# The mixer's convolution moved from TensorE, VectorE and ScalarE to GpSimd, with rows shifted by transfers inside the chip

## The reference

```python
x = x + 0.5 * ffn(layernorm(x), gate_weight, wi, wo)
n = layernorm(x)                                   # n_t: row of token t
t = conv_w[:,0]*n_{t-1} + conv_w[:,1]*n_t + conv_w[:,2]*n_{t+1} + conv_b   # per channel, zero beyond a batch's ends
u, v  = n @ Wu.T + bu, n @ Wv.T + bv
gates = sigmoid(relu(n @ Wg1.T + bg1) @ Wg2.T + bg2)
x = x + t + (cumsum(u*gates, axis=1) * (v*gates)) @ Wu
x = x + 0.5 * ffn(layernorm(x), gate_weight, wi, wo)
```

## Time and profile before

| | before |
|---|---|
| median of 3 runs (lowest to highest) | 1102.23 us (1101.32 to 1102.9) |
| the profiled execution's own time | 1102.27 us |
| its span | 1100.5 us |
| its granted TensorE clock | 0.973 |
| mixer, first transposition to its last products | 463.85 to about 656 us |

### The profile page before, as it was taken

How to read it: one execution, slowest core, us unless ns; L and a number is a source line. 1 busy time by engine, 2 the same in 40 slices (tenths; PEclk the granted TensorE clock), 3 DMA queues, 4 the chain that set the end, 5 groups by cost and what they waited for, 6 DMA issues and landing times.

```text
span 1100.5 us, 20918 instructions
## 1 busy us (share of the span) xinstructions
PE 1050.6 (95%) x7912; PEld 994.7 (90%) x7912; DVE 721.7 (66%) x1089; ACT 544.2 (49%) x851; POOL 147.0 (13%) x135
## 2 busy tenths in 40 slices
PE   8699999999999999599999996999999999999995
PEld 6699999999999999478777776999999999999995
DVE  7566566766677777388685874557767677665652
ACT  4445454665556575253333234355656656554431
POOL 2201111113020210100000022002112021130101
PEclk9699999999999999899999996999999999999998
DMA  8458646566465651500011235346566564654410
GB/s 307 175 229 287 204 142 216 182 232 211 166 211 185 243 198 55 177 1 1 1 39 39 77 105 179 128 149 243 178 226 233 193 243 178 227 212 143 170 38 24
DMA packets 83277, 177.33 MB, mean 161 GB/s; under 512 B 4192, under 2 KB 4704, under 8 KB 83168
## 3 DMA queue, kind: packets, MB, share of 16 engines
q1 hardware_dynamic: 75488, 152.61, 39.5%
q0 software_dynamic: 7168, 23.07, 5.9%
q10 hardware_dynamic: 576, 1.05, 0.3%
HBM read 162.04 MB, written 18.87 MB: 164 GB/s over the span
## 4 chain that ended last, share of the span: by engine, by line
PE 93%; ACT 1%; DMA 1%; DVE 1%; issue 1%; POOL 1%; POOLq 0%; SPq 0%; ACTq 0%; DVEq 0%
PE psH L1213 13%; PE psH L1212 13%; PE psH L1214 13%; PE acc L1220 12%; PE acc L1221 12%; PE acc L1219 12%; PE acc L1212 3%; PE acc L1214 3%; PE acc L1213 3%; PE psT L1428 1%; PE psT L1267 1%; PE psH L1340 1%; PE acc L1384 1%; PE psH L1384 1%; PE psT L1533 1%
## 5 line engine op out<-in xcount | busy, mean ns | idle before, releaser
L1212 PE MATMUL psH<-dth,wih 128*128 128x240 f32 (+5 forms) x1024 | 294.2, 287 | 0.0
L1213 PE MATMUL psH<-dtl,wih 128*128 128x240 f32 (+5 forms) x1024 | 293.3, 286 | 0.0
L1220 PE MATMUL acc<-htl,woh 128*128 128x240 f32 (+5 forms) x1024 | 293.3, 286 | 0.0
L1221 PE MATMUL acc<-hth,wol 128*128 128x240 f32 (+5 forms) x1024 | 293.1, 286 | 0.0
L1214 PE MATMUL psH<-dth,wil 128*128 128x240 f32 (+5 forms) x1024 | 293.0, 286 | 0.0
L1219 PE MATMUL acc<-hth,woh 128*128 128x240 f32 (+5 forms) x1024 | 293.0, 286 | 0.0
L786 DVE TENSOR_TENSOR wol<-raw_wo,woh 128x1024 fp32r<-128x1024 f32 x128 | 155.7, 1223 | 146.3 <-ACT woh L608 146.3
L642 ACT ACTIVATE gel<-psH 128x320 f32<-128x320 f32 x256 | 112.0, 437 | 188.3 <-PE psH L1214 183.0
L608 ACT ACTIVATE woh<-raw_wo 128x1024 fp32r<-128x1024 f32 x128 | 134.3, 1057 | 132.2 <-PE acc L1221 132.2
L1212 PEld LDWEIGHTS psH<-dth,wih 128*128 128x128 f32 x1024 | 193.5, 189 | 0.4
L1213 PEld LDWEIGHTS psH<-dtl,wih 128*128 128x128 f32 x1024 | 193.5, 189 | 0.0
(11 more groups left out here) (194 smaller groups left out, 1163.8 us busy)
## 6 DMA issues: line engine op xcount, KB each, us to landing
raw_wi<-in_wi SPq DMA_DIRECT2D x64, 1024.0 KB, 5.1
raw_wo<-in_wo SPq DMA_DIRECT2D x64, 1024.0 KB, 5.3
out_x<-xt SPq DMA_DIRECT2D x4, 1024.0 KB, 5.8
xt<-in_x SPq DMA_DIRECT2D x6, 512.0 KB, 7.8
xt<-x SPq DMA_DIRECT2D x3, 1024.0 KB, 9.7
raw_u<-in_wuT SPq DMA_DIRECT2D x1, 1024.0 KB, 10.9
raw_u<-in_wvT SPq DMA_DIRECT2D x1, 1024.0 KB, 12.6
xt<-in_x ACTq DMA_DIRECT2D x2, 256.0 KB, 3.4
```

The source lines that it names most:

```text
L1212: pe.matmul(out, lh, rh, start=first, stop=False)
L1213: pe.matmul(out, lh, rl, start=False, stop=False)
L1220: pe.matmul(out, lh, rl, start=False, stop=False, skip_group_check=True)
L1221: return pe.matmul(out, ll, rh, start=False, stop=False, skip_group_check=True)
```

## The change

The convolution is computed on the rows with tokens on partitions. A tile's row one token earlier or later lies on the next partition, so SP copies each group's `xn` twice inside the SBUF: into `late` one partition down (127 rows of four tiles) and into `soon` one partition up, with single rows for the edges. GpSimd multiplies `late`, `xn` and `soon` with rows of weights (`conv_row`), adds the bias and the three products and adds the sum to `xt`: 28 operations of 128x512 a group, with waits after each four. `conv_row` is made once, between the layers, by 16 transpositions on TensorE and 4 copies on ScalarE. `conv_mid`, `tap`, `turn_conv` and the first addition of `adds` are gone. `xn` has memory for two groups now, so that `norm(g)` for g >= 2 waits until GpSimd has added group g-2, and `adds(w)` waits for GpSimd's addition of tile w. `late` and `soon` exist once each.

```diff
+                    def shift(g):
+                        this = group_of(g)
+                        sp.wait_ge(n_xn, g + 1)
...
+                        if g % 2:
+                            sp.dma_start(soon[P - 1:P, GROUP - 1, :], this[0:1, 0, :]).then_inc(soon_edge, 16)
+                        sp.wait_ge(late_free, g + 1)
+                        sp.dma_start(late[1:P, :, :], this[0:P - 1, :, :]).then_inc(late_in, 16)
+                        sp.dma_start(late[0:1, 1:GROUP, :], this[P - 1:P, 0:GROUP - 1, :]).then_inc(late_in, 16)
+                        if g % 2:
+                            sp.wait_ge(row_held, 16 * (g // 2 + 1))
+                            sp.dma_start(late[0:1, 0, :], held_row).then_inc(late_in, 16)
+                        else:
+                            sp.dma_start(held_row, this[P - 1:P, GROUP - 1, :]).then_inc(row_held, 16)
+                        sp.wait_ge(soon_free, g + 1)
+                        sp.dma_start(soon[0:P - 1, :, :], this[1:P, :, :]).then_inc(soon_in, 16)
+                        sp.dma_start(soon[P - 1:P, 0:GROUP - 1, :], this[0:1, 1:GROUP, :]).then_inc(soon_in, 16)
+
+                    shift(0)
+                    shift(1)
+                    shift(2)
                     keep(0)
+                    shift(3)
                     keep(1)
-                    sp.wait_ge(d_conv, DC * GROUPS)
+                    sp.wait_ge(n_xTl, DC * GROUPS)
+                    sp.wait_ge(conv_added, TILES)
...
+            def convolve(g):
...
+                pool.wait_ge(late_in, 16 * (2 * (g + 1) + (g + 1) // 2))
+                each(late, late, by_row(0), ALU.mult, conv_step)
+                pool.wait_ge(soon_in, 32 * (g + 1))
+                pool.wait_ge(row_held, 16 * (g // 2 + 1))
+                pool.wait_ge(n_T, DC * (g + 1))
+                each(this, this, by_row(1), ALU.mult, conv_step)
+                pool.wait_ge(conv_step, step + 2 * GROUP)
+                each(this, this, by_row(3), ALU.add, conv_step)
+                pool.wait_ge(conv_step, step + 3 * GROUP)
+                each(this, this, late, ALU.add, conv_step)
+                pool.wait_ge(conv_step, step + 4 * GROUP)
...
+                    pool.sem_inc(late_free, 1)
...
+                each(soon, soon, by_row(2), ALU.mult, soon_scaled)
+                pool.wait_ge(soon_scaled, GROUP * (g + 1))
+                each(this, this, soon, ALU.add, conv_step)
+                pool.wait_ge(conv_step, step + 5 * GROUP)
...
+                    pool.sem_inc(soon_free, 1)
...
+                each(xt[:, q, :], xt[:, q, :], this, ALU.add, conv_added)
...
                     for g in range(GROUPS):
-                        power(g, slice(g * GROUP, (g + 1) * GROUP), n_var, n_rstd)
+                        if g + 1 < GROUPS:
+                            power(g + 1, slice((g + 1) * GROUP, (g + 2) * GROUP), n_var, n_rstd)
+                        convolve(g)
...
+                    if g >= 2:
+                        act.wait_ge(conv_added, GROUP * (g - 1))
...
-                    dve.wait_ge(p_conv, w + 1)
-                    dve.tensor_tensor(xt[:, w, :], psT[w % 2][:, :], xt[:, w, :], ALU.add).then_inc(d_addc, 1)
+                    dve.wait_ge(conv_added, w + 1)
                     dve.wait_ge(p_uv, w + 1)
-                    dve.wait_ge(d_addc, w + 1)
                     dve.tensor_tensor(xt[:, w, :], psH[w % 2][:, :], xt[:, w, :], ALU.add).then_inc(d_addu, 1)
...
+                pe.wait_ge(s.eoT_done, DC * (E + 1))
+                for k in range(4):
+                    for c in range(DC):
+                        col = CB0 + c if k == 3 else CW0 + 3 * c + k
+                        ins = pe.transpose(acc[k][:, c * P:(c + 1) * P], small[:, col:col + 1].to_broadcast([P, P]),
+                                           ident[:, :])
+                    ins.then_inc(rows_turned, 1)
```

More of the change, by code:

```diff
@@ L111, in build_kernel @@
         a_xn = top[0]
-        xn = put("xn", [P, TILES, D], F32)
+        xn = put("xn", [P, 2 * GROUP, D], F32)
+        late = put("late", [P, GROUP, D], F32)
+        soon = put("soon", [P, GROUP, D], F32)
         wu = [put(f"wu{k}", [P, DC, D], F32R) for k in "hl"]
@@ L176, in build_kernel @@
         top[0] = shared
-        xT = put("xT", [P, DC, SEQ + 2], F32)
+        xT = put("xT", [P, DC, GT], F32)
+        conv_row = put("conv_row", [P, 4, D], F32)
         glh = put("glh", [P, 2, DC, GT], F32R)
@@ L477, in gather, with by_row, each @@
                                             ).then_inc(gathered[a][k], 16)
+            def convolve(g):
+                this = group_of(g)
+                q = slice(GROUP * g, GROUP * g + GROUP)
+                def by_row(k):
+                    return conv_row[:, k, :].unsqueeze(1).to_broadcast([P, GROUP, D])
+                def each(out, one, two, op, done):
+                    for j in range(GROUP):
+                        pool.tensor_tensor(out[:, j, :], one[:, j, :], two[:, j, :], op).then_inc(done, 1)
+                step = 5 * GROUP * g
+                if g == 0:
+                    pool.wait_ge(rows_spread, 4)
+                pool.wait_ge(late_in, 16 * (2 * (g + 1) + (g + 1) // 2))
[9 more added lines that the diff above has]
+                pool.wait_ge(conv_step, step + 4 * GROUP)
+                if g % 2:
+                    pool.memset(late[0:1, 0, :], 0.0).then_inc(late_free, 1)
+                else:
+                    pool.sem_inc(late_free, 1)
+                    pool.wait_ge(soon_edge, 16 * (g // 2 + 1))
+                each(soon, soon, by_row(2), ALU.mult, soon_scaled)
+                pool.wait_ge(soon_scaled, GROUP * (g + 1))
+                each(this, this, soon, ALU.add, conv_step)
+                pool.wait_ge(conv_step, step + 5 * GROUP)
+                if g % 2:
+                    pool.sem_inc(soon_free, 1)
+                else:
+                    pool.memset(soon[:, GROUP - 1, :], 0.0).then_inc(soon_free, 1)
+                each(xt[:, q, :], xt[:, q, :], this, ALU.add, conv_added)
             s0 = layers[0]
@@ L707, in take_xT @@
                         act.wait_ge(n_xT, DC * g + c + 1)
[L708 to L716, removed]
+                        act.activation(xTh[g % 2][:, c, :], xT[:, c, :], copy).then_inc(n_xTh, 1)
                 def relu(g):
@@ L732, in _ @@
                 x1_tiles = x1[0:T, :].rearrange("(n p) d -> p n d", p=P)
+                act.wait_ge(s.wi_lo, STEPS * E)
+                for k in range(4):
+                    act.wait_ge(rows_turned, k + 1)
+                    act.activation(conv_row[:, k, :], acc[k][:, :], copy).then_inc(rows_spread, 1)
                 act.wait_ge(uv_lo, 2 * DC)
@@ L751, in _ @@
                             glob_hi(i - 1)
[L752 to L755, removed]
+                        if c == 0 and not more:
+                            copy_tiles(0, nxt)
                         if c == 1:
@@ L1523, in turn_group @@
                             ins = pe.transpose(to[:, j * P:(j + 1) * P],
-                                               xn[:, GROUP * g + j, c * P:(c + 1) * P], ident[:, :])
+                                               group_of(g)[:, j, c * P:(c + 1) * P], ident[:, :])
                         ins.then_inc(n_T, 1)
[L1527 to L1535, removed]
                 def times_wu(g, j):
```

72 lines of the change are left out of this document (29 added, 43 removed).

## The result

The changed kernel takes 1320.19 us (median of 3 runs, 1317.99 to 1321.21) where the kernel before takes 1102.23: a ratio of 1.1985, 95% interval 1.1965 to 1.2005. The profiled execution took 1321.21 us, with a span of 1319.5 and a mean granted clock of 0.895 (0.973 before). 1316 was predicted, in a range of 1284 to 1373.

The account below looks back on a forecast made before the run. TensorE's order of products set the pace; with the change, one-engine copies would. Tables end at 878.5 instead of 668.4 us, +210, and +3 for the gather: 1102.3 + 213.7 gives 1316 us, range 1284 to 1373.

Parts of the forecast that it names:

- One engine for 127 rows: Copies into `late` and `soon`: 127 rows run on one DMA engine, one copy after the other; 83% likely.
- equal shares: DMA transfers: rows are dealt equally over the engines, inferred from the store's 528 packets and the cut of single rows.
- The pace of one engine: Copies into `late` and `soon`: 1.04 MB on one engine takes 40 us, with bounds of 36 to 46.
- The period: Each group in the mixer: 12 operations at 1.0, two copies of 40 and 2 us for issue and landing, 94 us.
- The GpSimd operation: Convolution on GpSimd: 1.0 us for each 128x512 operation, between 0.91 at the least and 1.44 at the most.
- The last layer: GpSimd's queue: last `soon` lands at 830, so the last layer's first 1/sqrt moves from 640.26 to 854 us.
- The tail: From the last layer's first 1/sqrt to the end of the tables: 28 - 6.5 + 3 us, ending at 878.5.
- The +3 for the clock: Last layer: TensorE, idle for most of 200 us, starts again at a lower granted clock, +3 us.
- The saving: TensorE in the mixer: sixteen `turn_conv` removed free 7.1 us, plus 1 for holds; worth nothing while TensorE waits.
- The rival of sharing by sixteen: Copies into `late` and `soon`: shared by 16 engines, landing in 5 us; 1099 us, or 1112 at 1.15 an operation; 9%.
- the holds of GpSimd: GpSimd in the mixer: waiting for VectorE's two-input instructions lengthens its group from 28 to about 38 us.
- what comes late: Mixer, with copies shared by sixteen: 1.4 us for `norm(2)`, 2.3 at the turn to group 1, 1 later.

Follow-up runs that it names:

- e1: The changed kernel with each copy of 127 rows cut into two transfers, of 112 and 15 rows: 1121.39 us, ratio 1.0183 to the kernel before.
- e2: The changed kernel with each copy of 127 rows cut into two transfers, of 124 and 3 rows: 1122.73 us.
- e4: The changed kernel with each copy of 127 rows cut into two transfers, of 126 rows and one row: 1127.11 us.
- e7: The changed kernel with copies cut into 112 and 15 rows, each four GpSimd operations written as one of 128x2048, except additions to `xt`: 1161.98 us.
- e8: The changed kernel with copies cut into 112 and 15 rows and all 28 GpSimd operations a group left out: 1092.86 us, ratio 0.9910 to the kernel before.
- e6: The changed kernel with copies cut into 112 and 15 rows, GpSimd doing 16 operations a group instead of 28: 1103.66 us, ratio 1.0010 to the kernel before.
- e3: The changed kernel with only the copies into `soon` cut into 112 and 15 rows, `late` left at 127: 1199.83 us.

## Why the prediction was right, point by point

**One engine for 127 rows: right, and the deciding step.** The plateau at 27 GB/s, the cut copies of e1, e2 and e4 and the packet counts show it. The inference of equal shares, drawn from packet counts, holds for 124, 126 and 127 rows.

**The pace of one engine: 38.9 us a copy for 40.** The dragging ends at 27 GB/s in the earlier trace rows were the nearest row, and gave 38.5. Eight copies: -9.

**The period: 95.9 to 96.3 us for 94**, from two errors that nearly cancel: 12 operations took 15.0 us for 12 (+3), two copies 2.2 less, and issue and landing 3.1 for 2 (+1). That the period came out so near is luck in part. GpSimd waits for transfers for 57 us of it (24.75 + 32.49), not 66, since its own operations take longer.

**The GpSimd operation: 1.23 us for 1.0, the term that was mis-sized.** It was read from the `at_facts` products, and they were a poor row for it: in the changed kernel that of 1152 values again takes 2.14 us, 1.86 ns a value, while 512 values of plain tiles take 2.40 ns each. By e7 (4.56 us for 2048, above) an operation of plain tiles is 0.12 us and 2.17 ns a value, an estimate from these two sizes. The upper bound, 1.44, held it; the range's 1.15 did not. It cost 60 x 0.23 = 14 us. The Trainium skill (GPSIMD Engine Reference, section 3.1) gives 4497 ns for 2048 values, which agrees with the 4.56 us of e7; the 1.12 worked out from it was nearer than the row. What in `at_facts` makes it cheaper was not tried.

**The last layer: 1/sqrt at 863.2 for 854.** Last `soon` used at 832.8 for 830, and the 24 operations behind it 30.4 us for 24. `adds(0)` and `norm(2)` got free at about 571.6 and 577.0 (the first of four additions from 570.37, and the 1/sqrt behind them), for 567 and 573.

**The tail: 21.6 us from there to the end of the tables, for 24.6;** 884.8 for 878.5 in all. The +3 for the clock was too much: the granted clock was 0.50 while TensorE stood, 0.54 from 864 to 870 us and 1.00 from 870 to 885, and TensorE was busy for only 3.5 us of the first six. What follows took 436.4 us (1321.21 - 884.8), 2.5 more than before, for +3. The forecast's own addition is off by 0.6: 878.5 - 668.4 + 3 is 213.1, not 213.7, so its terms give 1315.4. The profiled execution of 1321.2 lies 5.8 us above that: 6.3 from the end of the tables, less 0.5. The 14 us of the GpSimd operations and the 9 of the copies go opposite ways, so 1316 is nearer to 1320 than its terms are to what they measured.

**Not foreseen, the late issue of `soon`.** It was to take up to 80 us from issue to landing. It took 60.6 (580.10 to 640.68), because SP issued it 20 us late (below). It cost nothing, since `soon` stood behind `late` on the same engine anyway.

**The saving: right, and worth nothing here.** 7.1 + 1 us were read from the earlier trace rows; e8 shows 8.9.

**The rival of sharing by sixteen** can be judged by e1, and its chances were split too kindly: 5 of its 9 in 100 lay on faster. Its own bound, an operation at 1.05 us, was passed, and its 1112 for 1.15 was the nearest of its figures to 1121. Its group of 38 us was 28 plus 10 of holds; measured are 44.5, that is 34.4 for 28 operations at 1.23, some 2 for the small ones, and 8 of holds. So the holds of GpSimd were priced about right, 10 for 8. Those of VectorE were not: about 3.4 us were put for what comes late, and e6 - e8 shows 10.8 for 16 operations a group alone. How e1's 28.5 us above e8 (1121.39 - 1092.86) split between GpSimd's full queue and later products stays open beyond that difference, since with 12 operations fewer the holds are fewer too. No version with the whole convolution beat the kernel before.

## What to carry to other kernels

Look at the number of rows of a transfer before its bytes: 127 rows took 38.9 us where the same bytes in 112 and 15 rows land in 5.2 to 5.4, and cutting 15 off took 199 us out of this kernel. Work that is moved to GpSimd is not free for VectorE: price each two-input instruction of VectorE by the length of the GpSimd instruction it may meet, keep those short, and ask whether GpSimd's queue also carries a small step that the next stage waits for. Take a price from a row with the same kind of operands, and where only an unlike one is there, let the range reach to its far bound.

## What the runs showed of the hardware that was not expected

**An issue on SP stands behind a one-engine transfer.** SP's timeline in the changed kernel:

```profile
559.81 0.63 SPq L386 DMA_DIRECT2D late<-xn  x1
560.48 18.40 SPq L387 DMA_DIRECT2D late<-xn  x1
578.93 1.13 SPq L390 DMA_DIRECT2D late<-lgT  x1
580.10 1.36 SPq L394 DMA_DIRECT2D soon<-xn  x1
581.51 34.44 SPq L395 DMA_DIRECT2D soon<-xn  x1
```

The issue of 127 rows takes 0.6 to 1.4 us, and the small one behind it 18.4, or 34.4 where two such copies are under way. It is so in all four groups, but for group 2, where the first small issue behind `late` took 0.53 and the second 17.86. In e3, where `soon` is cut, the issue behind it takes 1.71 and the one behind `late` still 17.34. Everything later in SP's order is held for that long, here the issue of `soon`. Why the issue stands was not tried, and no run prices it.

**GpSimd also holds a cast.** The cast `hh<-hid`, with one input, takes 422 ns in the kernel before and 888 in e1 (the mean of four, from 464 to 669 us). In e8, without the 28 operations, it takes 426, and in e7, with instructions four times as long, 1587. The prediction counted two-input instructions alone. The Trainium skill (SBUF — State Buffer, Who interferes with whom) lists casts among the one-input forms that can meet GpSimd when they run in a mode that takes both ports, which agrees.
